# A fused chain of four adapted linear layers: A3 and Wr are loaded, transposed and split ahead of W3's first block

## The reference

```
L0:  x W0^T + 0.5 (x A0[label0]) B0^T                       one adapter of several, picked for each batch entry
L1:  x Weff^T,  Weff = quantise(W1 + 0.5 B1 A1) + 0.5 B1 A1  codebook of 8 levels, scale per group of 128
L2:  x W2^T + 0.5 (x A2[label2]) B2^T
L3:  x W3^T + 2 * sum over 8 experts of gate_e (x A3_e^T) B3_e^T
     gate = softmax of the two largest of (x Wr^T + 5 * onehot(label7)), zero for the others
```

## Time and profile before

| | |
|---|---|
| Median of 3 runs | 683.54 us (682.65 to 684.33) |
| Profiled execution: span from first to last instruction | 680.7 us |
| Profiled execution: its own time | given as the span alone; the median is 2.8 us longer |
| TensorE busy | 671.0 us, 99% of the span |
| TensorE weight loads (beside the matmuls) | 617.6 us, 91% |
| VectorE busy | 339.6 us, 50% |
| ScalarE busy | 156.7 us, 23% |
| GpSimd busy | 89.1 us, 13% |
| DMA | 37.15 MB, mean 55 GB/s; 268 GB/s in the first of 40 slices |

### The profile page before, as it was taken

How to read it: one execution, slowest core, us unless ns; L and a number is a source line. 1 busy time by engine, 2 the same in 40 slices (tenths; PEclk the granted TensorE clock), 3 DMA queues, 4 the chain that set the end, 5 groups by cost and what they waited for, 6 DMA issues and landing times.

```text
span 680.7 us, 9276 instructions
## 1 busy us (share of the span) xinstructions
PE 671.0 (99%) x3504; PEld 617.6 (91%) x3504; DVE 339.6 (50%) x603; ACT 156.7 (23%) x241; POOL 89.1 (13%) x174
## 2 busy tenths in 40 slices
PE   6999999999999999999999999999999999999997
PEld 5999999989999999999999799999999999999996
DVE  2589989899988418100110483333333333333322
ACT  3432111361111226111210541111111111111111
POOL 2102125202202101100100121110011111111100
PEclk9999999999999999999999999999999999999999
DMA  9942133101100033212512011111111111120001
GB/s 268 207 110 88 38 62 63 32 1 31 32 1 0 1 51 50 32 31 31 62 31 63 1 41 55 60 62 43 49 62 62 62 62 62 62 62 31 33 32 62
DMA packets 93438, 37.15 MB, mean 55 GB/s; under 512 B 58396, under 2 KB 91164, under 8 KB 93412
## 3 DMA queue, kind: packets, MB, share of 16 engines
q1 hardware_dynamic: 93412, 36.79, 21.6%
HBM read 28.39 MB, written 8.39 MB: 54 GB/s over the span
## 4 chain that ended last, share of the span: by engine, by line
PE 98%; DMA 1%; DVE 0%; issue 0%; ACT 0%; POOL 0%; ACTq 0%; SPq 0%; DVEq 0%; POOLq 0%
PE acc L896 52%; PE acc L998 32%; PE acc L986 3%; PE acc L1039 3%; PE aux L937 2%; PE acc L1038 2%; PE aux L890 1%; PE acc L890 1%; PE aux L1030 1%; DMA g<-in_L_cond_W_dram 1%; PE aux L1029 0%; ACT out_sb L629 0%; POOL g L395 0%; ACTq L102 0%; DVE gate L863 0%
## 5 line engine op out<-in xcount | busy, mean ns | idle before, releaser
L896 PE MATMUL acc<-h_hi,w_hi 128*128 128x440 f32 (+2 forms) x576 | 144.6, 359 | 0.2 <-issue 0.2
L896 PE MATMUL acc<-h_hi,w_lo 128*128 128x440 f32 (+2 forms) x576 | 142.2, 355 | 0.0
L896 PE MATMUL acc<-h_lo,w_hi 128*128 128x440 f32 (+2 forms) x576 | 142.1, 355 | 0.0
L896 PEld LDWEIGHTS acc<-h_hi,w_hi 128*128 128x128 f32 x576 | 105.8, 188 | 7.1 <-issue 0.6
L896 PEld LDWEIGHTS acc<-h_lo,w_hi 128*128 128x128 f32 x576 | 107.0, 188 | 5.1
L896 PEld LDWEIGHTS acc<-h_hi,w_lo 128*128 128x128 f32 x576 | 106.6, 188 | 5.0
L998 PE MATMUL acc<-h_hi,xt_hi 128*128 128x408 f32 x384 | 99.5, 364 | 0.0
L998 PE MATMUL acc<-h_lo,xt_hi 128*128 128x408 f32 x384 | 94.0, 349 | 0.0
L998 PE MATMUL acc<-h_hi,xt_lo 128*128 128x408 f32 x384 | 93.5, 348 | 0.0
L998 PEld LDWEIGHTS acc<-h_hi,xt_lo 128*128 128x128 f32 x384 | 71.7, 188 | 0.4
L998 PEld LDWEIGHTS acc<-h_lo,xt_hi 128*128 128x128 f32 x384 | 71.6, 188 | 0.1
(11 more groups left out here) (155 smaller groups left out, 584.8 us busy)
## 6 DMA issues: line engine op xcount, KB each, us to landing
x_st<-in_x_dram SPq DMA_DIRECT2D x64, 128.0 KB, 2.9
out_dram<-out_sb SPq DMA_DIRECT2D x16, 512.0 KB, 2.7
g<-in_L_cond_W_dram SPq DMA_DIRECT2D x8, 512.0 KB, 7.1
w_st<-in_L_cond_W_dram SPq DMA_DIRECT2D x8, 512.0 KB, 5.4
w_st<-in_L_cond_weight_dram SPq DMA_DIRECT2D x8, 512.0 KB, 4.1
w_st<-in_L_cond_weight_dram SPq DMA_DIRECT2D x32, 128.0 KB, 3.3
g<-in_L_cond_lora_A_dram SPq DMA_DIRECT2D x5, 128.0 KB, 3.4
a_raw<-in_L_cond_lora_A_dram SPq DMA_DIRECT2D x20, 32.0 KB, 1.9
```

What stands on the lines that cost most here:

```text
L896: last = pe.matmul(acc[0:a.shape[-1], slot, bank * BANK:bank * BANK + c1 - c0], a[:, k, :], b[:, k, OFF + c0:OFF + c1], start=(k == 0 and ...
```

## The change

The loads of A3 and Wr, their sixteen transposes, their three casts and their three subtractions are each put ahead of the corresponding work for W3's block 0, on all four instruction streams. GpSimd's stream is unchanged, and so are all waits' counts.

```diff
@@ sync
+            sp.dma_start(w1_eff[:, 0].rearrange("p k i -> p (k i)"),
+                         A3.rearrange("e r d -> (e r) d")).then_inc(a3_in, 16)
+            sp.dma_start(w1_eff[0:E, 1].rearrange("p k i -> p (k i)"), Wr).then_inc(a3_in, 16)
             for k in range(KT):
                 sp.dma_start(g[:, :, k * P:(k + 1) * P], slices(W3)[:, :, k * P:(k + 1) * P]).then_inc(w3_in[k], 16)
                 if k == 0:
-                    sp.dma_start(w1_eff[:, 0].rearrange("p k i -> p (k i)"),
-                                 A3.rearrange("e r d -> (e r) d")).then_inc(a3_in, 16)
-                    sp.dma_start(w1_eff[0:E, 1].rearrange("p k i -> p (k i)"), Wr).then_inc(a3_in, 16)
                     sp.dma_start(w_st[:, 0], slices(W2)[:, :, 0:P]).then_inc(w_in[0], 16)
@@ scalar
+            act.wait_ge(a3_t, 1)
+            for bank, (k0, k1) in enumerate(a3_tiles):
+                act.copy(h_hi[:, k0:k1, OFF + C_H:OFF + C_LOW2], a3_at(bank, k0, k1)).then_inc(a3_hd, 1)
             for k in range(KT):
                 act.wait_ge(w3_t, k + 1)
                 act.copy(h_hi[:, k, OFF:OFF + D], w3_at(k)).then_inc(split_hi, 1)
                 if k == 0:
                     act.wait_ge(w_eye, 1)
                     act.copy(w_hi[:, 0], w_st[:, 0]).then_inc(w_hi_done, 1)
-                    act.wait_ge(a3_t, 1)
-                    for bank, (k0, k1) in enumerate(a3_tiles):
-                        act.copy(h_hi[:, k0:k1, OFF + C_H:OFF + C_LOW2], a3_at(bank, k0, k1)).then_inc(a3_hd, 1)
@@ vector
+            for bank, (k0, k1) in enumerate(a3_tiles):
+                cols = slice(OFF + C_H, OFF + C_LOW2)
+                dve.wait_ge(a3_hd, bank + 1)
+                dve.tensor_tensor(h_lo[:, k0:k1, cols], a3_at(bank, k0, k1), h_hi[:, k0:k1, cols].bitcast(F32),
+                                  ALU.subtract).then_inc(a3_done, 1)
             for k in range(KT):
                 dve.wait_ge(split_hi, k + 1)
                 dve.tensor_tensor(h_lo[:, k, OFF:OFF + D], w3_at(k), h_hi[:, k, OFF:OFF + D].bitcast(F32),
                                   ALU.subtract).then_inc(h_ready, 1)
                 if k == 0:
                     low(w_st[:, 0], 0, 1)
-                    for bank, (k0, k1) in enumerate(a3_tiles):
-                        cols = slice(OFF + C_H, OFF + C_LOW2)
-                        dve.wait_ge(a3_hd, bank + 1)
-                        dve.tensor_tensor(h_lo[:, k0:k1, cols], a3_at(bank, k0, k1), h_hi[:, k0:k1, cols].bitcast(F32),
-                                          ALU.subtract).then_inc(a3_done, 1)
@@ tensor
             pe.wait_ge(made, 2)
-            turn_w3(0)
             pe.wait_ge(a3_in, 32)
             for bank, (k0, k1) in enumerate(a3_tiles):
                 for k in range(k0, k1):
                     at = a3_at(bank, k0, k1)[:, k - k0]
                     turn_tile(at[:, 0:ER], w1_eff[:, 0, k, :])
                     last = turn_tile(at[:, ER:NR], w1_eff[0:E, 1, k, :])
             last.then_inc(a3_t, 1)
+            turn_w3(0)
             for k in range(KT):
                 if k + 1 < KT:
                     turn_w3(k + 1)
```

## The result

The changed kernel takes 684.57 us (median of 20 runs, 682.85 to 686.25), the kernel before 682.88 (20 runs, 682.23 to 684.33): ratio 1.0026, interval 1.0017 to 1.0034. The forecast was 684.5, in a range of 682.8 to 686.3, by +1.0 on a median of three runs that lay 0.66 above the median of twenty. So the time was met in part by luck: the base that I forecast from was 0.66 too high, and the difference, undersized by 0.7, made up for it.

A forecast was written before the change was run, and what follows sets the result against it. TensorE bounds the kernel, so the first product's start decides: T0 4.7, transposes 4.80 and 1.96, then the split tail give 15.0 against 14.01, +1.0 on a median of 683.54: 684.5 us, range 682.8 to 686.3.

The forecast's parts named there:

- T0: TensorE's first A3 transpose, once A3 and Wr land: 4.7 us, between 4.1 and 5.3.
- The loads behind: W3 blocks landing behind A3 and Wr: block 0 ready before 7.5, wanted at 9.5, hidden by 2 us; block 1 at 10.04.
- The tail: Four ScalarE and VectorE split steps for block 0 and W2, bare behind block 0's turn: 3.5 us, first product at 15.0.
- Rival D: Block 1's turn covers the four split steps, only the earlier start shows: -0.6 us, 682.9; chance 0.04.
- Rival C: A3 with Wr lands no sooner than W3 block 0 did, TensorE starts at 5.3: +1.6 us, 685.1; chance 0.09.
- The clock: TensorE's clock rise around the first products, taken as long after the first product as before: zero in the sum.
- the hole: TensorE idle between block 1's turn and the first product, 13.4 to 15.0: 1.6 us.
- Rival A: Denser transposes lift the clock early: +0.15 us, 683.7, or -0.95, 682.6, if ahead of block 0's turn; chance 0.12.
- rival B: Idle time before the products sets the clock's rise past block 2's turn: +2.6 us, 686.1; chance 0.14.

The follow-up runs named there:

- order_only: Changed kernel's compute order on all engines, with the loads in the order of the kernel before; 687.78 us, ratio 1.0065 to the kernel before.
- late_low: Changed kernel, but the first six products of tile 0 no longer wait for VectorE's W2 subtraction; 682.12 us, ratio 0.9994 to the kernel before.
- after_again: Changed kernel run once more with no edit, for another profiled execution; 684.46 us, ratio 1.0018 to the kernel before.
- late_low_fill: late_low with two unused identity transposes in what is left of its hole behind block 1's turn; 682.12 us, ratio 0.9984 to the kernel before.
- held_after: late_low_fill with fourteen unused identity transposes ahead of A3's; 681.95 us, ratio 0.9984 to the kernel before.
- loads_only: Kernel before with only the loads in the changed kernel's order, compute order unchanged; 685.68 us, ratio 1.0036 to the kernel before.
- warm_turns: Kernel before with fourteen unused identity transposes ahead of the first transpose; 682.58 us, ratio 0.9996 to the kernel before.
- held_after_full: held_after with sixteen more unused identity transposes between the turns of blocks 0 and 1; 681.63 us, ratio 0.9983 to the kernel before.
- held_before: Kernel before with unused identity transposes: fourteen ahead of block 0's turn, four behind it, eight behind A3's; 680.24 us, ratio 0.9963.
- warm_before: Kernel before with nine unused products ahead of the first transpose; 682.20 us, ratio 0.9990 to the kernel before.

## Why the prediction was right, and where it was short

**The start of TensorE.** Forecast T0 = 4.7 with 4.1 to 5.3; read 4.90, 5.18, 4.91, 5.46 and 5.05 in five profiles of this load order. Low by 0.2 to 0.8, 0.35 in the middle. The releaser is Wr, 3.36 us after its own issue at 1.40, so a nearly full landing for 32 KB was not generous, as I had called it; the truth lay between my value and the high bound in four of the five, and above the bound in one (5.46). The estimate from the Trainium skill's formula ("DMA: Bandwidth & Descriptors", 4.4) was further off than the row's.

**The loads behind.** Here the working failed, without cost. I had block 0 with its identity added before 7.5 and block 1 untouched at 10.04. In the profile GpSimd takes them at 8.15 and 11.48:

```profile
8.15 0.45 POOL L395 TENSOR_TENSOR g<-g,ident 128x128 f32<-128x128 f32 x1 [6.45 <-DMA g<-in_L_cond_W_dram]
...
11.48 0.46 POOL L395 TENSOR_TENSOR g<-g,ident 128x128 f32<-128x128 f32 x1 [1.20 <-DMA g<-in_L_cond_W_dram]
```

That left 1.1 us of slack for block 0 instead of 2, and TensorE waited 0.30 us for block 1, inside the later hole. The rates of the first microseconds differ from one execution to the next (GpSimd had block 0 at 7.03 and 7.86 in others); why is open.

**The tail.** T0 to first product was forecast as 10.3 and measured as 10.29, 10.28, 10.28 and, in order_only, 10.29. This is the core of the prediction, and late_low shows the cause: take out its last link and the start falls to 14.15. Rival D falls with it. Rival C (a start at 5.3) was nearly true in one execution (5.18) and true in another (5.46), and is part of the 0.35 above.

**The clock.** Two terms were short: T0, as above, and the clock, which I had set to zero. The changed kernel loses about 1.7 at the median. By an estimate from the two profiles (first product at 15.19 and 15.46) 1.2 to 1.5 of it is the start, and the rest, 0.2 to 0.5, is the clock. But that rest is the remainder of larger swings. With the hole filled, the clock is up at the first product, which repays 0.75 of the later start (683.08, level with before); with the hole open the median is 1.4 higher (684.46 to 684.57). Rival A and rival B, to which I gave 0.12 and 0.14, both show in the profiles. A rightly said that transposes count. In the first profile the clock was up within 0.3 us of the first product, with only transposes and the hole before it. B's late rise is in after_again, some 2.7 us behind the first product instead of 1.6, and my argument against B (the clock is low anyway, so nothing is dropped) was wrong: in order_only it had risen and was dropped. That the hole itself does the harm is likely, not shown. For it: late_low_fill's two transposes took off late_low's upper tail, and the falls in order_only and held_after came behind holes. Against it as the only reason: loads_only had its late rise without a hole, and in warm_turns and held_after_full the clock fell with no wait of TensorE longer than 0.42 us behind it since its first instruction. What sets the moment is open.

I had leaned on the Trainium skill's page "TensorE: Matmul & The Clock Gate", "Part 4: PE-mode transpose", by which the full clock does not engage for transposes. The turn in 1.09 us in warm_turns contradicts it, and the measurement decides. The rule in Part 1 of the same page of the Trainium skill, that activity lifts the throttle, fits that turn; but it does not tell why the 8.5 us of the kernel's own transposes in loads_only did not lift the clock and the 3.24 us of the identity in warm_turns did.

## What to carry to other kernels

Moving work to an engine's idle start only pays if what it used to cover is covered by something else: ask which short jobs ran under the moved block, and add up the chain that they form once they stand bare. Where that chain leaves TensorE idle just ahead of its products, price the hole twice, once as time and once as clock; unused transposes of the identity in such waits are a cheap test. In the kernel before they were the winning edit (held_before); in the changed order, with a fixed number of them, they missed (held_after_full). With a few tenths of a per cent at stake, look at the spread and its groups before the median, and at two or more profiles.

## What the runs showed of the hardware that I had not expected

- The column of the granted clock reads 1.00 from the start of the trace until the first fall is recorded, while products and transposes run at half speed (0.32 us for 388 columns, 0.24 us a transpose). Only after a fall does it read 0.50. The spacing of equal instructions is the safer reading.
- Dense transposes can lift the clock (fourteen of them, 3.24 us, in warm_turns). A3's group, pairs of a 128-row and an 8-row transpose, does not reliably hold it: the clock fell amid it in warm_turns (8.2 us), at its end in warm_before (10.8 us) and 0.6 us behind it in held_after_full (9.1 us), though TensorE counts as busy all through the group. In held_before it held.
- Where a fall of the clock came behind a hole, it came well after it: in order_only 1.6 us after a hole of 1.78 us, in held_after 1.1 us after one of 2.04 us. Look for the hole ahead of a fall, and do not count on finding one: in loads_only the clock was late without any.
